# Splitting the rows of B once into a DRAM scratch tensor, in a fused two-layer adapter kernel

## The reference

```python
def _L0(x, conditions, weights):            # weights: (200, 64, 64)
    w = weights[conditions]
    return jnp.einsum('bct,bcd->bdt', x, w)

def _L1(x, W, A, Bm, scalings, adapter_idx): # A: (8, 16, 512), Bm: (8, 512, 16)
    H = jnp.einsum('btd,od->bto', x, W)
    xa = jnp.einsum('btd,brd->btr', x, A[adapter_idx])
    delta = jnp.einsum('btr,bor->bto', xa, Bm[adapter_idx])
    return H + delta * scalings[adapter_idx][:, None, None]

x = x + _L0(x, itok_B_1_198, L0_weights)
x = x + _L1(x, W, A, Bm, scalings, itok_B_0_6)
```

## Time and profile before

| | us |
|---|---|
| median of 3 runs | 78.05 |
| lowest and highest run | 77.72, 78.56 |
| span of the profiled execution | 76.0 |
| TensorE busy in it | 71.5 |
| VectorE busy | 55.2 |
| ScalarE busy | 51.4 |
| GpSimd busy | 33.6 |

### The profile page before, as it was taken

One profiled execution on the slowest core, in us unless ns is written; L12 is line 12 of the kernel. 1 busy time (PEld: TensorE's weight loads), 2 busy tenths in 40 slices (PEclk: granted clock), 3 DMA queues, 4 the chain that ended last, 5 costly groups with the idle time before them and its releaser, 6 DMA issues.

```text
span 76.0 us, 1936 instructions
## 1 busy us (share of the span) xinstructions
PE 71.5 (94%) x464; PEld 65.1 (86%) x464; DVE 55.2 (73%) x144; ACT 51.4 (68%) x126; POOL 33.6 (44%) x76
## 2 busy tenths in 40 slices
PE   3989999999999999999999999999999999999940
PEld 3957887785999699999999999999999999999930
DVE  4007954987979797979597968977797949675920
ACT  0725956995896597686768666968687767567440
POOL 5700591499799906354354515580655260000000
PEclk9999999999999999999999999999999999999999
DMA  0899479436789989578967963579416430303025
GB/s 0 208 417 390 118 213 236 142 113 205 234 284 281 306 276 294 210 243 225 302 207 214 311 220 70 151 201 312 156 39 237 138 138 4 138 13 138 0 97 179
DMA packets 9677, 14.55 MB, mean 191 GB/s; under 512 B 3650, under 2 KB 4418, under 8 KB 9666
## 3 DMA queue, kind: packets, MB, share of 16 engines
q1 hardware_dynamic: 7554, 9.16, 36.9%
q0 software_dynamic: 1536, 4.20, 18.4%
q10 hardware_dynamic: 576, 1.07, 4.5%
HBM read 10.23 MB, written 4.19 MB: 190 GB/s over the span
## 4 chain that ended last, share of the span: by engine, by line
PE 71%; DMA 9%; DVE 5%; issue 5%; ACT 4%; POOL 1%; POOLq 0%; ACTq 0%
PE z_ps L653 45%; PE z_ps L641 9%; DMA head<-head_a 5%; DMA b_raw<-b_t 4%; PE out_ps L708 4%; PE out_ps L709 3%; PE out_ps L695 3%; PE out_ps L713 3%; PE v_ps L687 2%; DVE b_stack L521 2%; DVE a_table L590 1%; ACT out_sb L413 1%; ACT a_table L427 1%; ACT x_high L387 1%; POOL b_raw L287 1%
## 5 line engine op out<-in xcount | busy, mean ns | idle before, releaser
L653 PE MATMUL z_ps<-moving,x_high 128*128 128x272 f32 x224 | 33.5, 290 | 0.0
L653 PEld LDWEIGHTS z_ps<-moving,x_high 128*128 128x128 f32 x224 | 29.9, 188 | 0.6
L287 POOL DMA_DIRECT2D b_raw<-b_t x32 | 16.1, 506 | 11.3 <-issue 5.2
L653 PE MATMUL z_ps<-moving,x_low 128*128 128x272 f32 x112 | 18.6, 288 | 0.0
L280 POOL CAST moving<-a_table 128x128 fp32r x28 | 9.1, 355 | 17.0 <-PE z_ps L653 14.3
L653 PEld LDWEIGHTS z_ps<-moving,x_low 128*128 128x128 f32 x112 | 15.8, 188 | 0.0
L512 DVE TENSOR_TENSOR z_low<-z_ps,z_high 128x272 fp32r<-128x272 f32 (+1 forms) x28 | 11.8, 422 | 1.4 <-ACT z_high L364 0.5
L521 DVE TENSOR_TENSOR b_stack<-b_raw,b_high 128x512 fp32r<-128x512 f32 x16 | 11.9, 741 | 0.2 <-ACT b_high L380 0.2
L380 ACT ACTIVATE b_high<-b_raw,group_sb 128x512 fp32r<-128x512 f32 x16 | 11.5, 716 | 0.2 <-DMA b_raw<-b_t 0.2
L364 ACT ACTIVATE z_high<-z_ps 128x272 fp32r<-128x272 f32 (+1 forms) x28 | 10.5, 376 | 0.2
L394 ACT ACTIVATE v_high<-v_ps,group_sb 128x128 fp32r<-128x128 f32 x16 | 5.8, 366 | 7.0 <-PE v_ps L687 6.9
(11 more groups left out here) (59 smaller groups left out, 76.6 us busy)
## 6 DMA issues: line engine op xcount, KB each, us to landing
b_raw<-b_t POOLq DMA_DIRECT2D x32, 128.0 KB, 3.2
out<-out_sb SPq DMA_DIRECT2D x15, 256.0 KB, 3.0
x_raw<-xt SPq DMA_DIRECT2D x13, 256.0 KB, 3.8
w_sb<-w SPq DMA_DIRECT2D x32, 16.0 KB, 3.1
w_late<-w_late_t SPq DMA_DIRECT2D x1, 480.0 KB, 6.9
head<-head_c ACTq DMA_DIRECT2D x1, 400.0 KB, 4.7
head<-head_d SPq DMA_DIRECT2D x1, 384.0 KB, 5.7
head<-head_a ACTq DMA_DIRECT2D x1, 264.0 KB, 3.5
```

The source lines that it names most:

```text
L287: pool.dma_start(b_raw[s * C:(s + 1) * C, t % BBUFS, :], b_t[ds(which[s], 1), :, :].rearrange("a r (g n) -> (a r) g n", g=1) .to_broadcast ...
L653: last = nc.tensor.matmul(z_bank(t, part), x[:, t % XBUFS, k * P:(k + 1) * P], moving[:, int(n == HL), k, at:at + HALF], start=((n, k) == ...
```

## The change

The eight adapters' 16 rows of B, 128 rows in all, are loaded once into `b_rows`, split once into `b_rows_high` (ScalarE) and `b_rows_low` (VectorE), and stored to an internal DRAM tensor `b_split` of shape (adapter, rank, group, 512): the low rows into group 0, the high rows three times into groups 1 to 3. `LOW_B` becomes 0. ScalarE issues the load (as its fourth) and the store of the high rows, SyncE that of the low rows. From tile 2 on `load_b` reads its 64 rows for a sample from `b_split` straight into `b_stack`, which gets four buffers in place of two; `high_of_b` and `low_of_b` stay for tiles 0 and 1 alone, from `b_raw` with `load_raw_b`. GpSimd waits for both stores ahead of `load_b(2)`; from tile 4 on `load_b(t)` waits for `out_done` of tile t - 4. `add_low_rank` waits for the load itself.

```diff
-    LOW_V, LOW_B, LOW_U = 1, 2, 3
+    LOW_V, LOW_B, LOW_U = 1, 0, 3
...
-        b_raw = sb("b_raw", [P, BBUFS, OUT], fp32)
-        b_high = sb("b_high", [P, 2, OUT], fp32r)
-        b_stack = sb("b_stack", [P, 2, OUT], fp32r)
+        b_raw = sb("b_raw", [P, PLAIN, OUT], fp32)
+        b_high = sb("b_high", [P, PLAIN, OUT], fp32r)
+        b_rows = sb("b_rows", [ADAPTERS * RANK, OUT], fp32)
+        b_rows_high = sb("b_rows_high", [ADAPTERS * RANK, OUT], fp32r)
+        b_rows_low = sb("b_rows_low", [ADAPTERS * RANK, OUT], fp32r)
+        b_stack = sb("b_stack", [P, BBUFS, OUT], fp32r)
+
+        b_split = nc.dram_tensor("b_split", [ADAPTERS, RANK, GROUPS, OUT], fp32, kind="Internal").ap()
...
@@ SyncE
             load_w0(which[3], 3)
+            sync.wait_ge(b_rows_low_ready, 1)
+            sync.dma_start(b_split[:, :, LOW_B, :].rearrange("a r n -> (a r) n"),
+                           b_rows_low[:].bitcast(fp32)).then_inc(b_low_written, 16)
             for t in range(4, TILES):
...
@@ GpSimd
             def load_b(which, t):
 
                 if t >= BBUFS:
-                    pool.wait_ge(b_stack_ready, t - BBUFS + 1)
+                    pool.wait_ge(out_done, t - BBUFS + 1)
                 for s in range(PER):
-                    pool.dma_start(b_raw[s * C:(s + 1) * C, t % BBUFS, :],
-                                   b_t[ds(which[s], 1), :, :].rearrange("a r (g n) -> (a r) g n", g=1)
-                                   .to_broadcast([RANK, GROUPS, OUT]),
+                    pool.dma_start(b_stack[s * C:(s + 1) * C, t % BBUFS, :].bitcast(fp32),
+                                   b_split[ds(which[s], 1), :, :, :].rearrange("a r g n -> (a r g) n"),
                                    ).then_inc(b_loaded[t % BBUFS], 16)
...
             add_identity(BATCH_OF[3])
+            pool.wait_ge(b_high_written, 16)
+            pool.wait_ge(b_low_written, 16)
             load_b(which[2], 2)
             take_a(which[3], 3)
             load_b(which[3], 3)
...
@@ ScalarE
             act.dma_start(a_scales[:], a_t).then_inc(a_loaded, 16)
+            act.dma_start(b_rows[:], b_t.rearrange("a r n -> (a r) n")).then_inc(b_rows_loaded, 16)
...
             high_of_w(3)
+            act.wait_ge(b_rows_loaded, 16)
+            nc.scalar.activation(b_rows_high[:], b_rows[:], ACT.Copy).then_inc(b_rows_high_ready, 1)
+            act.wait_ge(b_rows_high_ready, 1)
+            act.dma_start(b_split[:, :, LOW_B + 1:, :].rearrange("a r g n -> (a r) g n"),
+                          b_rows_high[:].bitcast(fp32).rearrange("p (g n) -> p g n", g=1)
+                          .to_broadcast([ADAPTERS * RANK, GROUPS - 1, OUT])).then_inc(b_high_written, 16)
             take_raw_a(1)
...
             high_of_v(2)
-            high_of_b(2)
...
-                high_of_b(t)
...
-            high_of_b(last)
...
@@ VectorE
             low_of_w(2)
+            dve.wait_ge(b_rows_high_ready, 1)
+            nc.vector.tensor_tensor(out=b_rows_low[:], in0=b_rows[:], in1=b_rows_high[:].bitcast(fp32),
+                                    op=ALU.subtract).then_inc(b_rows_low_ready, 1)
             dve.wait_ge(own_rank_ready, 2 + PER)
             take_low_rank(0)
...
-            low_of_b(2)
...
-                low_of_b(t)
...
-            low_of_b(last)
...
@@ TensorE
             def add_low_rank(t, dst, col, n, stop):
                 pe.wait_ge(v_ready, t + 1)
-                pe.wait_ge(b_stack_ready, t + 1)
-                return nc.tensor.matmul(dst, v_stack[:, t % 2, :], b_stack[:, t % 2, col:col + n],
+                if t < PLAIN:
+                    pe.wait_ge(b_stack_ready, t + 1)
+                else:
+                    pe.wait_ge(b_loaded[t % BBUFS], 16 * PER * ((t - PLAIN) // BBUFS + 1))
+                return nc.tensor.matmul(dst, v_stack[:, t % 2, :], b_stack[:, t % BBUFS, col:col + n],
                                         start=False, stop=stop)
```

More of the change, by code:

```diff
@@ L129, in adapted_residual_kernel @@
         a_loaded = sem("a_loaded")
+        b_raw_loaded = [sem(f"b_raw_loaded{t}") for t in range(PLAIN)]
+        b_rows_loaded = sem("b_rows_loaded")
+        b_rows_high_ready = sem("b_rows_high_ready")
+        b_rows_low_ready = sem("b_rows_low_ready")
+        b_high_written = sem("b_high_written")
+        b_low_written = sem("b_low_written")
         b_loaded = [sem(f"b_loaded{i}") for i in range(BBUFS)]
@@ L280, in take_a, with load_raw_b @@
                     nc.gpsimd.tensor_copy(dst, src.bitcast(fp32)).then_inc(a_cols_ready, 1)
+            def load_raw_b(which, t):
+                for s in range(PER):
+                    pool.dma_start(b_raw[s * C:(s + 1) * C, t, :],
+                                   b_t[ds(which[s], 1), :, :].rearrange("a r (g n) -> (a r) g n", g=1)
+                                   .to_broadcast([RANK, GROUPS, OUT]),
+                                   ).then_inc(b_raw_loaded[t], 16)
             def load_b(which, t):
                 if t >= BBUFS:
-                    pool.wait_ge(b_stack_ready, t - BBUFS + 1)
+                    pool.wait_ge(out_done, t - BBUFS + 1)
                 for s in range(PER):
-                    pool.dma_start(b_raw[s * C:(s + 1) * C, t % BBUFS, :],
-                                   b_t[ds(which[s], 1), :, :].rearrange("a r (g n) -> (a r) g n", g=1)
-                                   .to_broadcast([RANK, GROUPS, OUT]),
+                    pool.dma_start(b_stack[s * C:(s + 1) * C, t % BBUFS, :].bitcast(fp32),
+                                   b_split[ds(which[s], 1), :, :, :].rearrange("a r g n -> (a r g) n"),
                                    ).then_inc(b_loaded[t % BBUFS], 16)
@@ L303, in _ @@
             pool.wait_ge(a_loaded, 16)
-            load_b(which[0], 0)
-            load_b(which[1], 1)
+            load_raw_b(which[0], 0)
+            load_raw_b(which[1], 1)
             add_identity(0)
@@ L375, in high_of_b @@
             def high_of_b(t):
[L377 to L380, removed]
+                act.wait_ge(b_raw_loaded[t], 16 * PER)
+                nc.scalar.activation(b_high[:, t, :], b_raw[:, t, :], ACT.Copy,
                                      scale=group_sb[:, LOW_B:LOW_B + 1]).then_inc(b_high_ready, 1)
@@ L518, in low_of_b @@
                 dve.wait_ge(b_high_ready, t + 1)
[L519 to L522, removed]
+                nc.vector.tensor_tensor(out=b_stack[:, t, :], in0=b_raw[:, t, :],
+                                        in1=b_high[:, t, :].bitcast(fp32),
                                         op=ALU.subtract).then_inc(b_stack_ready, 1)
```

## The result

The changed kernel takes 78.86 us (median of 5 runs, 78.3 to 79.22) against 78.05: a ratio of 1.0166 with a 95% interval of 1.0112 to 1.022. Run again later, beside its variants, it came out at 1.0083 (1.0043 to 1.0122). So it is slower, by 1.7% in one comparison and by 0.8% in the other. The profiled execution has a span of 76.6 us, 0.6 more than the one before; it was the fastest of its runs.

A forecast was written before the change was run, and what follows sets the result against it. TensorE's gap-free matmuls from 27.07 us were taken to bound the kernel. -0.3 (tile 3's stall) + 0.1 (head) + 0.25 (take_a(3) late) = +0.05 us on 78.05 gave 78.1 us, range 77.5 to 79.4.

The forecast's parts named there:

- the likeliest case: Time within 1% of no change, chance 0.70; as forecast within half a microsecond, 0.60.
- The steady part: TensorE's gap-free matmuls from 27.07 us stay at 4.04 us a tile; work removed behind there is worth 0.
- The removal: Dropping ScalarE's copies and VectorE's subtractions ends tile 3's stall ahead of tile 4's low-rank product: -0.3 us.
- The bound on the gain: TensorE loses only 0.3 us to other engines after 18.93, so no gain above this is to be had.
- The last wait before 27 us: TensorE's wait until 26.69, tile 4's low-rank product waiting for VectorE, was to be gone.
- The head's own work: Load of B's rows, ScalarE's copy and issue, VectorE's subtraction fit into idle time: 0.1 us booked.
- The stores: Both DRAM stores landed by 17.2, so GpSimd starts load_b(2) at 17.3 instead of 16.05, 1.25 us late.
- take_a(3): On GpSimd, ends at 18.95 to 19.3; TensorE wanted it for a_bank(3) at 18.93: +0.25 us.
- The step that failed: GpSimd's queue behind load_b(2), 8.0 us without waits, shrinks to 7.15 and ends at 24.45; z_high at 25.25 is in time.
- Late stores: Rival: each microsecond the later store lands behind 16.95 delays a_bank(3) by one; over 1% slower from about 17.95; chance 0.24.
- The B rows of tile 2 late: Rival: tile 2's B rows land at 23.1, 0.95 us behind TensorE's need: 79.1 us; chance 0.04.
- The head sticks out: Rival: late w_late and a 1.13 us issue on ScalarE delay take_raw_a(1) by 0.6 us: 78.6 us; chance 0.06.

The follow-up runs named there:

- e3: Changed kernel without B's table, split, stores and wait; later rows loaded into an unread buffer, product uses rows of tiles 0 and 1: 76.93 us, ratio 0.9886.
- e2: Kernel before plus the head's load, split and stores of B's rows, which nobody reads; every tile still splits its own rows: 78.68 us, ratio 1.009.
- e11: Changed kernel with table, split and stores kept but unread, no GpSimd wait; product uses rows of tiles 0 and 1: 77.71 us, ratio 0.9993.
- e8: Changed kernel storing 512 KB instead of 1 MB, high rows once, loaded into all four groups; waits kept: 77.32 us, ratio 0.9973.
- e4: Changed kernel with the high rows' store issued twice, second into a spare tensor, GpSimd waiting for both: 80.44 and 81.02 us, ratio 1.0367.
- e5: Changed kernel with GpSimd reading the indices of tiles 4 and 5 ahead of add_identity of tiles 2 and 3: 78.0 us, ratio 1.0044.
- e6: Changed kernel with add_identity of tiles 4 and 5 right behind take_a(4) on GpSimd: 77.75 us, ratio 1.0046.
- e1: Changed kernel with B's rows of tiles 2 and 3 still split on the spot, GpSimd's wait behind tile 3's loads: 79.37 us, ratio 1.0178.
- e9: Changed kernel with ScalarE's copy and store of the high rows moved ahead of high_of_w(2) and (3): 78.91 us, ratio 1.0159.
- e10: Changed kernel with e9's early store, the GpSimd edits of e5 and e6, and take_a(3) ahead of add_identity of tiles 2 and 3: 78.48 us, ratio 1.0116.

## Why the prediction was right or wrong

The measured 78.86 us lies in the range (77.5 to 79.4), but the sum, +0.05 us, was short of the measured +0.8. Slower by over 1% had been given 0.26, within 1% 0.70. By the first comparison (1.7%) the likeliest case was wrong; by the second (0.8%) it holds. That the time fell into the range owes more to the range's width than to the mechanism: the cost that was paid stood in no term.

*The steady part: right.* 4.04 us a stage before and after, and nothing gained behind 27 us.

*The removal: right in kind, perhaps too small.* -0.3 forecast, 0.4 us in e3's trace, but about 0.9 us by e3's ratio and by e2 against e11. The bound on the gain that the prediction took from the trace is thus not confirmed. The last wait before 27 us was to go; in the changed kernel the one for `z_high`, until 26.11, took its place. The busy time fell by about 8 us on each engine and not 9.5: an instruction starts some 0.1 us before the one ahead of it has ended, and busy time counts the overlap once, so fourteen instructions less are, I suppose, not fourteen full durations.

*The head's own work: right.* B's rows landed 6.3 us after their issue at 2.27, at 8.6; ScalarE's copy and issue took 0.61 and 0.41 us and fitted into the idle time, which shrank from 1.56 to 0.66; the mark did not move back. It came 0.24 us earlier than in the one trace before; the marks of the other runs lie on both sides of it, so I don't count this as a gain.

*The stores: the start of `load_b(2)` was right by luck.* The later store was forecast to land at 17.2 and `load_b(2)` to begin at 17.3. It landed at 16.5 and `load_b(2)` began at 17.23: the landing was put 0.7 us too late, and between it and the load stood not 0.1 but 0.7 us, in which the sequencer made the load ready. The sign named for being right, idle time that ends on a DMA at 17.2, did not appear. The Trainium skill ("DMA: Bandwidth & Descriptors", "Anatomy of one DMA") gives, for a DMA issued by GpSimd, a fixed 2.0 us plus bytes over 436 GB/s: 3.8 us for the 768 KB store by that estimate. These stores were issued by ScalarE and SyncE; the trace has 4.4 under this traffic and 2.1 for 256 KB alone, where that rule would give 2.6.

*`take_a(3)`: right.* Forecast to end at 18.95 to 19.3, it ended at 18.95, and `a_bank(3)` began at 19.00.

*The step that failed* is the sentence on GpSimd's queue further on: "ran from 16.05 to 24.07 without a wait to speak of, 8.0 us", less 0.87, "so the queue ends at ... 24.45". It ended at 25.37, 0.9 us later, although it had started on time (17.23). The time given back was right: from `load_b(4)` to the end of the identity it is 3.82 us, and was 4.71. The error lies ahead of it: from `load_b(2)` to `load_b(4)` it was 3.31 us (16.05 to 19.36) and became 4.32 (17.23 to 21.55). I had summed the engine's durations. The sequencer in front of it has work of its own: about 0.5 us for each DMA before the engine takes it up, and 1.3 us (19.60 to 20.9) to read four indices. In the kernel before it did that ahead of the engine, and only a gap of 0.48 us showed ahead of `load_b(4)`; that gap, which the prediction passed over, was the sign that the lead did not quite suffice even there. After a stop there is nothing to hide the reads behind. In the traces that keep the reads at their place `load_b(4)` begins about 1.9 us after they do: 17.5 and 19.36 before, 19.6 and 21.55 in the changed kernel, 18.8 and 20.69 in e2, 18.2 and 20.10 in e8. With 25.37 in place of 24.45, `z_high` ends at 26.11, which is what TensorE waited for: the forecast 25.25 plus the missing 0.9.

*What was left out* is what the stores do to other transfers. I priced the traffic beside them only as a delay of the stores. The reverse, a delay of `w0` of tile 3 (4.4 us to landing; up to 3.3 for the same loads before), was not in the sum. By e3 and e11 it costs as much as the wait. It reached TensorE by several ways, the queue of GpSimd in the changed kernel, the rows of B of tile 2 in e2 and tile 2's low-rank product in e11, so that the step above accounts for what the changed kernel's two traces show and not for every execution.

*The rivals.* "Late stores" was built on a landing after 17.95 and was not what happened in the changed kernel's traces, but e4 shows its slope of one for one, and e5's trace has `a_bank(3)` waiting behind a landing at 17.2 already. "The B rows of tile 2 late" did not occur in the changed kernel's traces, and did in e6's. "The head sticks out" did not occur. The rival that was missing: the wait ends on time and its queue is late all the same. What stays open: how much of the wait's 1% belongs to the loads of tiles 2 and 3 from the scratch tensor, which no run has without the wait, and why e1 is as slow as it is.

## What to carry to other kernels

A queue whose engine shows no idle time can still be near its limit: before a wait is put into it, sum the sequencer's work (index reads, the issue part of each DMA) from the waiting point to the next instruction that another engine needs, and not the engine's busy time alone. A burst of stores in a head full of loads has two prices, its own landing and the later landing of the small loads issued beside it; both may arrive at the same waiting instruction. And taking 8 us off each of two engines beside a bound third one was worth about 0.9 us here by the ratio, and 0.4 in the one trace.

## What the runs showed of the hardware

A DMA issued by GpSimd appears in two halves, and the first is hidden only while the sequencer is ahead. In the changed kernel's chain the first half is the 0.50 and 0.51 us called issue (16.70, 17.31, 21.02), between the sequencer's last register instruction and the engine's start, and the second the 0.52 us of each row on the engine. The Trainium skill (the same page and section) puts the sequencer's dispatch at some 50 ns and the making of descriptors, apart from it, at a small and variable time; here the two together take 0.5 us. A load from another queue came later because of a large store: `w0`'s second load for tile 3, issued at 11.40, 0.2 us behind the store, took 4.4 us, and with half the bytes stored 3.1 to 3.2. The first, issued at 10.8, ahead of the store, took 3.1 us, no longer than the 3.0 to 3.3 of the kernel before. The issues came slower too, where they met the store: in the two kernels that issue it earlier, e9 and e10, SyncE's four issues from 9.4 on took 3.87 and 3.48 us, and 2.44 in the others.
